# Attention layers of a four-layer graph network: probabilities turned by transfers inside SBUF and VectorE block transposes, contexts one slot later

## The chip, the cores and the metric

One core of a Trainium2 chip runs the whole program in one launch. The metric is the device time of that launch in microseconds, lower is better. The kernel before takes 2639.49 us, the median of 3 runs (2638.67 to 2640.51). The core has TensorE (PE; its weight loads are PEld), VectorE (DVE), ScalarE (ACT), GpSimd (POOL), and SyncE (SP), which issues nearly all transfers. Each engine works through its own instructions in order, and they meet at semaphores.

## The reference

The input is x of 128 graphs with 64 nodes and 384 features in float32, and an adjacency matrix of 64 x 64 for each graph. Four layers follow each other, each as x = layernorm(x + layer(x)). The first two are graph convolutions and stay as they are. The third and the fourth are the attention layers with 12 heads of 32 features:

```python
# third layer
q = (x @ Wq.T) ; k = (x @ Wk.T) ; v = (x @ Wv.T + bv)          # split in 12 heads
a = einsum('bnhd,bmhd->bhnm', q, k) * 384**-0.5 + adj[:, None]
pad = all(a == 0, axis=-1)                                     # rows that are all zero give zero
a = nan_to_num(softmax(where(pad, -inf, a)))
out = einsum('bhnm,bmhd->bnhd', a, v).reshape(...) @ Wo.T + bo
# fourth layer
q = x @ Wq + bq ; k = x @ Wk + bk ; v = x @ Wv + bv            # split in 12 heads
s = q k^T / sqrt(32) + beta * adj ; s = where(adj > 0, s, -9e15)
out = softmax(s) @ v
```

## The kernel before

`heads_pass` computes both attention layers as one pipeline of 32 slots. A slot is a group of 8 graphs, that is 512 rows in 4 tiles t of 128 rows; slots 0 to 15 are the third layer (`project(n)` is true, because that layer has the output projection Wo), slots 16 to 31 the fourth. There are three chunks c of 128 features, four heads each, and six units k of scores (`UNITS`), two for a chunk. Products that need full precision are done as three float32r products of high and low parts (`hhi`, `hlo`, `whi`, `wlo`).

For one slot: 54 matmuls of 128x512 make queries and keys (`query_key(n, k)`, k = 0 to 5: even k are queries, odd k are keys, in two ring banks of PSUM); 36 matmuls make the values (`value(n, t)`) in the same two ring banks; `chunk_scores(n, c)` makes the scores of four heads in a pair of banks. VectorE adds the adjacency while it takes the scores out, and reduces them to row maxima (`maxima`, L1725 to L1733); GpSimd subtracts these (`take_off`, L1890); ScalarE takes the exponential (`exponential`, L1619). TensorE turns the probabilities with six transposes for each tile (`probs_turned`, L1495) into two banks, ScalarE copies them to SBUF (`probs_out`, L1633), and TensorE multiplies them with the values (`output`, L1509), a column of ones giving the sums. VectorE divides (`divide`, L1766 to L1770). In the third layer the contexts are turned (`outputs_turned`), split into high and low parts and multiplied with Wo (`result`), and `result_out` adds them to the rows of x; then mean, variance and the final scaling follow (`final_stats`, `final_power` on GpSimd, `final_shift`, `final_apply` on ScalarE), and SP stores the rows.

The order of the work is written out by hand for each engine, in one loop over the slots n. On TensorE a slot holds: values of slot n, with the turned contexts of slot n-1 in between; the last chunk's scores of slot n; the Wo products of slot n-1; then the queries and keys of slot n+1, and between them the transposes, the contexts of slot n and the first two chunks' scores of slot n+1. VectorE takes the values out with their bias (`values_out`, 16 additions of 64x192 in a slot, L1745), turns the next strip of x with a block transpose (`rows_turned`, L1710), and does what is named above. ScalarE takes queries and keys out of PSUM (L1604, L1606, L1609) and makes the high parts (L1596); GpSimd makes the low parts (`low_parts`, L1897) and adds the bias or the contexts to the rows of x (`residual`, L1904, L1907). SP's queue holds for each slot: load of x, two loads of the adjacency, four loads of strips (each into 32 partitions, L1383), and the store of the slot before.

The rule for a new query projection is in its first wait; a bank of the ring is free again when the values of tile 2 (k = 0) or 3 (k = 1) have been taken out:

```python
            if k >= 2:
                pe.wait_ge(qk_evac, 2 * KC * n + k - 1)
            elif project(n - 2):
                pe.wait_ge(w_evac, T * (n - 2) + (1, 4)[k])
            else:
                pe.wait_ge(v_evac, max(T * (n - 1) + 3 + k, 0))
```

Of the kernel before, what the change touches and what calls it, by code (L numbers as in the profile page):

```python
# [13 lines left out]
P = 128  # L14
S = 64
# [1248 lines left out]
def heads_pass(nc, sh, ctx, rows, groups, x_ins, strip_ins, x_outs, adj_d, rowvec_d, colvec_d, beta_d):  # L1264
# [48 lines left out]
    q = sb("q", [P, KC, R])  # L1313
    keys = sb("keys", [P, KC, GRAPHS, 2, S])
    z = [sb(f"z{a}", [P, T, D]) for a in "ab"]
    at_low += [sh.rows_at + (KC * R + KC * GRAPHS * 2 * S + 2 * T * D) * 4]
    xt += [sb("xtb", [P, KC, R])]
    hlo = [placed(at)(f"hlo{a}", [P, KC, R], F32R) for at, a in zip(at_low, "ab")]
    logits = sb("logits", [P, KC, HP, T, S])
    val = sb("val", [P, GRAPHS, PAIRS, 2, HO])  # L1320
    sb = placed(sh.rows_end_at)
    rowvec = sb("rowvec", [P, 3, D])
    adjp = [sb(f"adjp{a}", [P, T, S]) for a in "ab"]
    probs = [sb(f"prob{a}", [P, KC, T, HP, S]) for a in "ab"]
    probt = [sb(f"probt{k}", [P, PAIRS, P]) for k in range(2)]
    o = sb("o", [P, T, D])
    at_ohi = sh.rows_end_at + (3 * D + 2 * T * S + 2 * KC * T * HP * S + 2 * PAIRS * P + T * D) * 4
# [3 lines left out]
    off = sh.stage[1][:, 0, 0:T * S].rearrange("p (t j) -> p t j", t=T)  # L1331
    pt, ot, ring = sh.bank[0:2], sh.bank[2:4], sh.bank[4:6]
    scores = sh.pair[:, :].rearrange("p (h t j) -> p h t j", h=HP, t=T)
    FV, FR, FB = (small[:, k, :] for k in range(3))

    output_banks = (pt[0], pt[1], ot[0], ot[1])
    result_banks = (ring[0], ot[1], ot[0], ring[1])
# [19 lines left out]
    exp_done = sem("exp_done")  # L1357
    pt_done = sem("pt_done")
    pt_evac = sem("pt_evac")
# [17 lines left out]
    def sync_program(sync):  # L1377
# [11 lines left out]

        def load_adj(n):  # L1390
            for b in range(2):
                sync.dma_start(adjp[n % 2][S * b:S * b + S, :, :], adj_d[b][n % groups])\
                    .then_inc(adj_loaded[n % 2], 16)
# [23 lines left out]
        load_x(1)  # L1417
        yield
# [12 lines left out]
        store(slots - 1)  # L1431
# [3 lines left out]
    def tensor_program(pe):  # L1435
        def query_key(n, k):
# [3 lines left out]
            elif project(n - 2):  # L1440
                pe.wait_ge(w_evac, T * (n - 2) + (1, 4)[k])
            else:
                pe.wait_ge(v_evac, max(T * (n - 1) + 3 + k, 0))
# [26 lines left out]
        def chunk_scores(n, c):  # L1470
            pe.wait_ge(qk_evac, 2 * KC * n + 2 * c + 2)
            pe.wait_ge(s_evac, UNITS * n + 2 * c)
            for t in range(T):
                for b in range(2):
                    g, out = 2 * t + b, slice(S * b, S * b + S)
                    for r in range(2):
                        heads = slice(S * r, S * r + S)
                        mm = nc.tensor.matmul(scores[out, 2 * r:2 * r + 2, t, :], q[heads, c, g * S:(g + 1) * S],  # L1478
                                              keys[heads, c, g, :, :],
# [3 lines left out]
        def probs_turned(n, t):  # L1483
            prob = probs[n % 2]
            pe.wait_ge(exp_done, UNITS * n + 2 * KC - 1 + t // 2)
            for half in range(2):
                if t:
                    pe.wait_ge(pt_evac, 2 * (T * n + t) - 1 + half)
                else:
                    pe.wait_ge(pt_evac, 2 * T * n)  # L1490
                    if project(n - 1):
                        pe.wait_ge(olo_done, T * (n - 1) + half + 1)
                for j in range(PAIRS // 2):
                    m = PAIRS // 2 * half + j
                    mm = nc.tensor.transpose(pt[half][:, j * P:(j + 1) * P],  # L1495
                                             prob[:, m // 2, t, m % 2 * 2:m % 2 * 2 + 2, :].rearrange("p h j -> p (h j)"),
                                             sh.ident[:, :])
                mm.then_inc(pt_done, 1)

# [622 lines left out]
```

## Time and profile before

| | |
|---|---|
| median of 3 runs | 2639.49 us |
| the profiled execution | 2636.74 us, its span 2634.8 us |
| TensorE matmuls | 2568.1 us busy, 97% of the span, 23040 matmuls |
| TensorE weight loads | 2234.6 us, 85% |
| VectorE | 2010.6 us, 76% |
| ScalarE | 1220.0 us, 46% |
| GpSimd | 1525.9 us, 58% |
| SP's DMA queue | 253008 packets, 184.21 MB, 25.6% of 16 DMA engines |
| granted TensorE clock, mean | 0.993 |

The profile is of one execution. Busy times of the engines lie beside each other. Matmuls are pipelined, so the modelled end of one lies beyond the start of the next, and the distance between two starts tells what one costs in a row of them. An idle time stands in square brackets with what ended it. A clock of 1.00 is 2.4 GHz, one of 0.50 is 1.2 GHz; a value between them is a mean over both levels. The attention layers take the last 1065 us of the span.

### The profile page before, as it was taken

The numbers are of one execution on the slowest core, as the hardware profiler recorded it, in microseconds if no ns is written. First come the engines' busy times: TensorE is split into PE (matmuls) and PEld (weight loads), VectorE is DVE, ScalarE is ACT, GpSimd is POOL, SyncE is SP. The second block draws the span as 40 slices with busy tenths as digits, with TensorE's granted clock in tenths as the row PEclk, the third lists the DMA queues.
The fourth block names the chain that finished last, engine by engine and source line by source line (L and its number), as shares of the span: only waits on it lengthen the run. The fifth ranks groups of instructions, "written<-read, shape, count | busy, mean of one in ns | idle before, by whom it ended". The sixth has DMA issues, their size and how long they took to land.

```text
span 2634.8 us, 59176 instructions
## 1 busy us (share of the span) xinstructions
PE 2568.1 (97%) x23040; PEld 2234.6 (85%) x23040; DVE 2010.6 (76%) x4485; ACT 1220.0 (46%) x2385; POOL 1525.9 (58%) x1380
## 2 busy tenths in 40 slices
PE   7999999999998999999999998999999999999997
PEld 7998998998996788888888877888888888888886
DVE  5788888888887667666666758888888877777776
ACT  2344344444343344344344444555455555556554
POOL 7657657656757667666667656444434435555553
PEclk9999999999999999999999999999999999999999
DMA  5112112112125222222222223312333323333432
GB/s 161 35 43 63 64 43 71 56 45 68 52 54 169 50 65 60 61 61 73 61 54 64 61 60 104 77 52 65 77 77 77 76 61 84 87 77 89 103 77 75
DMA packets 253285, 187.97 MB, mean 71 GB/s; under 512 B 175568, under 2 KB 250960, under 8 KB 253008
## 3 DMA queue, kind: packets, MB, share of 16 engines
q1 hardware_dynamic: 253008, 184.21, 25.6%
q8 instruction: 183, 3.00, 0.5%
q14 instruction: 94, 0.77, 0.1%
HBM read 133.84 MB, written 50.33 MB: 70 GB/s over the span
## 4 chain that ended last, share of the span: by engine, by line
PE 92%; DVE 3%; issue 2%; POOL 1%; ACT 1%; DMA 0%; POOLq 0%; ACTq 0%; DVEq 0%
PE bank L1449 15%; PE bank L344 14%; PE bank L1457 12%; PE bank L888 12%; PE pair L888 11%; PE pair L1478 4%; PE bank L1509 4%; PE bank L1495 4%; PE bank L326 3%; PE pair L326 3%; PE bank L359 2%; PE bank L874 2%; PE bank L912 2%; PE pair L912 2%; PE bank L374 1%
## 5 line engine op out<-in xcount | busy, mean ns | idle before, releaser
L1890 POOL TENSOR_TENSOR h_logits<-h_logits,h_mx 128x512 f32<-128x512 f32 x192 | 202.4, 1055 | 267.1 <-DVE h_mx L1733 267.1
L1745 DVE TENSOR_TENSOR h_val<-bank,h_rowvec 64x192 f32<-64x192 f32 x512 | 181.8, 355 | 33.3 <-PE bank L1457 24.4
L1185 POOL TENSOR_TENSOR l_hlo<-l_hf,l_hhi 128x576 fp32r<-128x576 f32 x96 | 134.8, 1433 | 115.0 <-ACT l_hhi L1005 115.0
L412 ACT ACTIVATE l_sides<-bank 128x512 f32<-128x512 f32 x192 | 113.0, 595 | 177.9 <-PE bank L344 177.9
L1449 PE MATMUL bank<-h_hhia,whi 128*128 128x512 f32 x450 | 185.9, 413 | 3.4 <-DVE h_hloa L1716 2.3
L1449 PE MATMUL bank<-h_hhia,wlo 128*128 128x512 f32 x450 | 177.4, 394 | 0.0
L1609 ACT ACTIVATE h_keys<-bank,h_keycol,h_halves 128x512 f32<-128x512 f32 x192 | 138.9, 776 | 83.0 <-PE bank L1449 83.0
L1082 DVE TENSOR_TENSOR l_val<-bank,l_vec 64x384 f32<-64x384 f32 x256 | 142.3, 556 | 40.3 <-PE bank L888 37.3
L1082 DVE TENSOR_TENSOR l_val<-pair,l_vec 64x384 f32<-64x384 f32 x256 | 142.3, 556 | 32.0 <-PE pair L888 28.3
L1224 POOL TENSOR_TENSOR l_vdiag<-l_vdiag,l_vec 128x384 f32<-128x384 f32 x128 | 127.8, 1019 | 66.0 <-ACT l_vdiag L986 66.0
L888 PE MATMUL bank<-whi,l_hhi 128*128 128x384 f32 x576 | 141.2, 353 | 5.8 <-POOL wlo L74 5.8
L1633 ACT ACTIVATE h_probt<-bank 128x384 f32<-128x384 f32 x256 | 111.5, 490 | 67.6 <-PE bank L1495 67.5
L663 POOL TENSOR_TENSOR l_small<-l_small,power 128x4 f32<-128x4 f32 x32 | 32.4, 1014 | 180.3 <-DVE l_small L524 180.3
L1005 ACT ACTIVATE l_hhi<-l_hf 128x576 fp32r<-128x576 f32 x96 | 58.6, 673 | 162.3 <-PE pair L888 159.2
L1733 DVE TENSOR_REDUCE h_mx<-h_logits 128x8 f32<-128x512 f32 x192 | 130.8, 681 | 3.3
L888 PE MATMUL pair<-whi,l_hhi 128*128 128x384 f32 x576 | 130.8, 334 | 1.5 <-DVE l_val L1082 1.5
L888 PE MATMUL bank<-wlo,l_hhi 128*128 128x384 f32 x576 | 131.8, 336 | 0.0
L888 PE MATMUL bank<-whi,l_hlo 128*128 128x384 f32 x576 | 131.3, 335 | 0.0
L888 PE MATMUL pair<-whi,l_hlo 128*128 128x384 f32 x576 | 131.0, 334 | 0.0
L888 PE MATMUL pair<-wlo,l_hhi 128*128 128x384 f32 x576 | 130.7, 334 | 0.0
L888 PEld LDWEIGHTS bank<-whi,l_hhi 128*128 128x128 f32 x576 | 97.4, 189 | 30.6 <-issue 18.6
L1509 PEld LDWEIGHTS bank<-h_val,h_probt 128*64 128x64 f32 x3072 | 95.2, 137 | 22.7 <-issue 22.7
(268 smaller groups left out, 7723.2 us busy)
## 6 DMA issues: line engine op xcount, KB each, us to landing
h_strips<-x SPq DMA_DIRECT2D x128, 192.0 KB, 5.1
l_hf<-xt SPq DMA_DIRECT2D x16, 864.0 KB, 4.7
l_x<-x SPq DMA_DIRECT2D x32, 384.0 KB, 3.2
h_za<-x SPq DMA_DIRECT2D x16, 768.0 KB, 4.8
h_zb<-x SPq DMA_DIRECT2D x16, 768.0 KB, 5.1
l_x<-x SPq DMA_DIRECT2D x15, 768.0 KB, 4.6
x<-l_zfa SPq DMA_DIRECT2D x8, 768.0 KB, 3.5
x<-l_zfb SPq DMA_DIRECT2D x8, 768.0 KB, 4.3
```

What stands on the lines that cost most here:

```text
L326: mm = nc.tensor.matmul(value_bank(n, k)[:, 0:D], hh[:, c, k * P:(k + 1) * P], ww[:, c, :], start=(j == 0), stop=(j == len(terms) - 1))
L344: mm = nc.tensor.matmul(ring[k % RING][:, :], ww[:, c, m * P:(m + 1) * P], hh[:, c, :], start=(j == 0), stop=(j == len(terms) - 1))
L888: mm = nc.tensor.matmul(ring[k % RING][:, 0:D], hh[:, c, first:first + P], ww[:, c, :], start=(j == 0), stop=(j == len(terms) - 1))
L1082: ins = nc.vector.tensor_tensor(val[half, (g + b) % GRAPHS, 0:D], ring[k % RING][half, 0:D], bias[half, :], ALU.add)
L1185: nc.gpsimd.tensor_tensor(hlo[:, c, :], hf[:, c, :], hhi[:, c, :], ALU.subtract).then_inc(lo_done, 1)
L1449: mm = nc.tensor.matmul(ring[k % 2][:, :], ww[:, c, m * P:(m + 1) * P], hh, start=(c == 0 and j == 0), stop=(c == KC - 1 and j == 2))
L1457: mm = nc.tensor.matmul(out, lhs, rhs, start=(j == 0), stop=(j == len(terms) - 1))
L1509: mm = nc.tensor.matmul(ot[t % 2][rows, 2 * m * HO:2 * (m + 1) * HO], probt[t % 2][:, m, rows], val[:, 2 * t + b, m, :, :].rearrange("p h ...
L1609: ins = nc.scalar.activation(keys[:, c, :, h, :], ring[1][:, :].rearrange("p (g j) -> p g j", j=S), ACT.Identity, scale=halves[:, h:h + 1] ...
L1733: nc.vector.tensor_reduce(mx[:, c, :, ts], row, AX.X, ALU.max)\
L1745: ins = nc.vector.tensor_tensor(val[S * p:S * p + S, 2 * t + b, :, p, 0:HD], src[rows, :, p, :], bias[rows, :, p, :], ALU.add)
L1890: nc.gpsimd.tensor_tensor(row, row, mx[:, c, :, ts].unsqueeze(3).broadcast_to([P, HP, 2, S]), ALU.subtract).then_inc(sub_done, 1)
```

## The change

The probabilities are no longer turned on TensorE. Scores, logits and adjacency get another layout: a row's 64 columns are split into two halves of 32, and the columns are laid out as (pair m, piece v, tile t, 32). The exponentials are written over the logits (there are two logits buffers now, and no `probs`). When all six exponentials of a slot are done, SP issues 16 transfers from SBUF to SBUF (`load_pieces`): each moves the 32x32 blocks of one of four groups of 32 partitions and one of four pieces (32 partitions, 6 x 128 float32 in a partition). VectorE then turns the blocks with four block transposes of 128x768 (`probs_turned`), which write `probt` for all four tiles.

The contexts of slot n are made at the start of slot n+1, all four tiles in a row in four banks, and the last chunk's scores of slot n+1 come right behind them, ahead of its values. Queries and keys of two chunks at a time are held instead of three. The values are taken out of PSUM by ScalarE without a bias, 16 copies a slot; the bias is added by GpSimd (`outputs_in`, to the contexts in the third layer, and `biases`, to the rows of x). GpSimd subtracts the maxima in two halves for each unit. The strips are turned one slot earlier (`rows_turned(n + 2)`) and so loaded one earlier; the adjacency is loaded in four parts.

```diff
+        def load_pieces(n):
+            sync.wait_ge(exp_done, UNITS * (n + 1))
+            sync.wait_ge(pt_done, T * n)
+            for v in range(STRIPS):
+                for w in range(P // SQ):
+                    sync.dma_start(pieces[SQ * v:SQ * v + SQ, w, :, :, :].rearrange("p m t a -> p m (t a)"),
+                                   logits[n % 2][SQ * w:SQ * w + SQ, :, v, :, :].rearrange("p m t a -> p m (t a)"))\
+                        .then_inc(pieces_loaded, 16)
...
         for n in range(slots):
-            if n >= 2:
-                load_x(n)
             if n and n + 1 < slots:
                 sync.wait_ge(s_evac, UNITS * n)
                 load_adj(n + 1)
-            if n + 2 < slots:
-                sync.wait_ge(xt_done, n + 2)
-                load_strips(n + 2)
+            load_pieces(n)
+            if n + 3 < slots:
+                sync.wait_ge(xt_done, n + 3)
+                load_strips(n + 3)
             if n:
                 store(n - 1)
+                if n + 1 < slots:
+                    load_x(n + 1)
...
         def output(n, t):
-            pe.wait_ge(pt_evac, 2 * (T * n + t + 1))
+            pe.wait_ge(pt_done, T * n + t + 1)
             pe.wait_ge(v_evac, T * n + t + 1)
...
         for n in range(slots):
             before, more = project(n - 1), n + 1 < slots
             if n:
+                for t in range(T):
+                    output(n - 1, t)
+                chunk_scores(n, 2)
                 value(n, 0)
...
             value(n, 2)
             value(n, 3)
-            chunk_scores(n, 2)
+            if n == 0:
+                chunk_scores(0, 2)
...
             if more:
                 query_key(n + 1, 0)
                 query_key(n + 1, 1)
-            if not before and more:
+                chunk_scores(n + 1, 0)
                 query_key(n + 1, 2)
-            probs_turned(n, 0)
...
                 query_key(n + 1, 3)
-            output(n, 0)
-            output(n, 1)
-            if more:
                 chunk_scores(n + 1, 1)
...
                 query_key(n + 1, 4)
-            probs_turned(n, 3)
-            if more:
                 query_key(n + 1, 5)
-            output(n, 2)
-            output(n, 3)
+        for t in range(T):
+            output(slots - 1, t)
```

The new order on ScalarE, GpSimd and VectorE (lines of the new loop; `alone` is true for n up to 16):

```python
        for n in range(slots):                    # ScalarE
            if n:
                exponential(n, 2)
                exponential(n, 3)
                if more and not alone:
                    high_parts(n + 1)
                values_out(n, 0)
            if before:
                outputs_high(n - 1, range(0, 2))
            if n:
                values_out(n, 1)
                exponential(n, 4)
            if before:
                outputs_high(n - 1, range(2, 4))
            values_out(n, 2)
            if n:
                exponential(n, 5)
            values_out(n, 3)
            if more and alone:
                high_parts(n + 1)
            if n == 0:
                for k in range(2, UNITS):
                    exponential(0, k)
            if more:
                query_key(n + 1, 0)
                query_key(n + 1, 1)
            if n:
                final_apply(n - 1)
            if more:
                query_key(n + 1, 2)
                query_key(n + 1, 3)
                exponential(n + 1, 0)
                exponential(n + 1, 1)
                query_key(n + 1, 4)
                query_key(n + 1, 5)

        for n in range(slots):                    # GpSimd
            if n and more and not alone:
                low_parts(n + 1)
            if n:
                outputs_in(n - 1)
            take_off(n, 4)
            take_off(n, 5)
            if n and more and alone:
                low_parts(n + 1)
...
            if n:
                final_power(n - 1)
            biases(n)
            if more:
                for k in range(4):
                    take_off(n + 1, k)
```

On VectorE a slot is now: the four divisions of slot n-1, two units of maxima, `outputs_low`, `rows_turned(n + 2)`, `result_out`, the final statistics, two units of maxima of slot n+1, and then in the third layer the four block transposes and two more units of maxima, in the fourth layer the two units first and the transposes after them.

## Rows read from the trace of the kernel before

**Rows 1.** Page, part 1: busy time, share of the span, instructions of each engine.
```profile
PE 2568.1 (97%) x23040; PEld 2234.6 (85%) x23040; DVE 2010.6 (76%) x4485; ACT 1220.0 (46%) x2385; POOL 1525.9 (58%) x1380
```

**Rows 2.** Windows, fourth layer: length, busy time of each engine, clock, DMA share, GB/s.
```profile
2200.00:2400.00 200.00, 200.00 (x2146) 169.47 (x2145) 153.41 (x351) 117.66 (x212) 105.67 (x98) 1.00 0.35 89
```

**Rows 3.** Timeline of TensorE: start, length (us), engine, line, operation, tiles, shape, count.
```profile
1629.48 0.80 PE L1457 MATMUL bank<-whi,h_hhia 128*128 128x384 f32 x3
...
1665.32 0.80 PE L1457 MATMUL bank<-whi,h_hhia 128*128 128x384 f32 x3
...
2202.92 0.80 PE L1457 MATMUL bank<-whi,h_hhia 128*128 128x384 f32 x3
...
2229.86 1.63 PE L1509 MATMUL bank<-h_val,h_probt 128*64 128x66 f32 x48
2231.41 0.80 PE L1457 MATMUL bank<-whi,h_hhib 128*128 128x384 f32 x3
...
2238.19 1.10 PE L1478 MATMUL pair<-h_keys,h_q 64*64 64x128 f32 x32
2239.22 0.50 PE L1449 MATMUL bank<-h_hhia,whi 128*128 128x512 f32 x1
```

**Rows 4.** Timeline of all engines, around a key projection in the third layer.
```profile
1760.13 0.64 PEld L1495 LDWEIGHTS bank<-ident,h_proba 128*128 128x128 f32 x6 [0.17 <-issue]
...
1762.47 0.39 PE L1449 MATMUL bank<-h_hlob,whi 128*128 128x512 f32 x1
...
1762.70 0.40 PE L1449 MATMUL bank<-h_hhia,wlo 128*128 128x512 f32 x1
...
1763.13 1.45 ACT L1609 ACTIVATE h_keys<-bank,h_keycol,h_halves 128x512 f32<-128x512 f32 x2 [1.48 <-PE bank L1449]
...
1764.63 1.10 PE L1478 MATMUL pair<-h_keys,h_q 64*64 64x128 f32 x32
```

**Rows 5.** Timelines of ScalarE and GpSimd, start of a fourth-layer slot.
```profile
2202.47 1.44 ACT L1609 ACTIVATE h_keys<-bank,h_keycol,h_halves 128x512 f32<-128x512 f32 x2
...
2203.30 1.99 POOL L1907 TENSOR_TENSOR h_za<-h_za,h_o 128x384 f32<-128x384 f32 x2 [3.56 <-DVE h_o L1770]
2205.55 3.79 POOL L1897 TENSOR_TENSOR h_hloa<-h_xta,h_hhib 128x512 fp32r<-128x512 f32 x3 [0.25 <-ACT h_hhib L1596]
```

**Rows 6.** Groups of instructions: busy us, mean ns of one, idle before and its releaser.
```profile
L1633 ACT ACTIVATE h_probt<-bank 128x384 f32<-128x384 f32 x256 | 111.5, 490 | 67.6 <-PE bank L1495 67.5
L1619 ACT ACTIVATE h_probb<-h_logits 128x512 f32<-128x512 f32 x96 | 58.9, 633 | 50.3 <-POOL h_logits L1890 49.7
L458 ACT ACTIVATE l_e<-l_ut 128x256 f32<-128x256 f32 x32 | 13.4, 418 | 148.2 <-DVE l_ut L504 148.2
L1890 POOL TENSOR_TENSOR h_logits<-h_logits,h_mx 128x512 f32<-128x512 f32 x192 | 202.4, 1055 | 267.1 <-DVE h_mx L1733 267.1
L629 POOL TENSOR_TENSOR l_maska<-l_adjna,tri 128x256 f32<-128x256 f32 x16 | 12.2, 763 | 0.0
L1710 DVE STREAM_TRANSPOSE h_xta<-h_strips 128x1536 f32<-128x1536 f32 x7 | 12.4, 1768 | 0.0
```

**Rows 7.** Second layer: two waits in TensorE's timeline, and windows behind them.
```profile
858.00 0.53 PE L374 MATMUL bank<-l_val,l_dt 64*64 64x385 f32 x1 [1.72 <-DVE l_dt L510]
...
885.50 0.53 PE L374 MATMUL bank<-l_val,l_dt 64*64 64x385 f32 x1 [3.59 <-DVE l_dt L510]
...
858.00:865.00 7.00, 7.00 (x40) 5.12 (x41) 4.54 (x19) 3.19 (x7) 1.02 (x1) 1.00 0.19 41
885.50:892.00 6.50, 6.50 (x31) 4.17 (x32) 3.90 (x16) 2.35 (x5) 1.02 (x1) 0.74 0.59 133
```

**Rows 8.** Line L1383: issue time in ns (min/median/max), and time to landing.
```profile
L1383 SPq DMA_DIRECT2D h_strips<-x x128: 303/546/2590, 1527.6 to 2551.6; - x128
...
DMA to landing us min/median/max: 2.9/5.1/6.8
```

**Rows 9.** Timeline of TensorE, entry to the attention layers.
```profile
1605.80 1.99 PE L1478 MATMUL pair<-h_keys,h_q 64*64 64x128 f32 x32 [5.51 <-DVE h_logits L1725]
```

More of the change, by code:

```diff
@@ L1330, in heads_pass @@
     olo = sb("olo", [P, T, KC, P], F32R)
-    off = sh.stage[1][:, 0, 0:T * S].rearrange("p (t j) -> p t j", t=T)
-    pt, ot, ring = sh.bank[0:2], sh.bank[2:4], sh.bank[4:6]
-    scores = sh.pair[:, :].rearrange("p (h t j) -> p h t j", h=HP, t=T)
+    off = sh.stage[1][:, 0, 0:T * S]
+    output_banks, ring = sh.bank[0:4], sh.bank[4:6]
+    scores = sh.pair[:, :].rearrange("p (m v t a) -> p m v t a", m=2, v=STRIPS, t=T)
     FV, FR, FB = (small[:, k, :] for k in range(3))
-    output_banks = (pt[0], pt[1], ot[0], ot[1])
-    result_banks = (ring[0], ot[1], ot[0], ring[1])
     vec_in = sem("vec_in")
@@ L1654, in scalar_program @@
             exponential(0, k)
-        high_parts(1)
-        for a in range(2):
-            act.wait_ge(rows.stored[a], 16 * (groups // 2))
         for n in range(slots):
             before, more = project(n - 1), n + 1 < slots
+            alone = n <= groups
             if n + 1 == groups:
@@ L1870, in vector_program @@
                 final_shift(n - 1)
+            else:
+                for a in range(2):
+                    dve.wait_ge(rows.stored[a], 16 * (groups // 2))
             if more:
@@ L1878, in vector_program @@
                 maxima(n + 1, 3)
-        divide(slots - 1, 2)
-        divide(slots - 1, 3)
+            if not project(n):
+                for t in range(T):
+                    probs_turned(n, t)
+        for t in range(T):
+            divide(slots - 1, t)
         final_stats(slots - 1)
@@ L1919, in gpsimd_program @@
         take_off(0, 3)
+        pool.wait_ge(vec_in, 16 * 3)
         for n in range(slots):
-            before, more = project(n - 1), n + 1 < slots
+            more, alone = n + 1 < slots, n <= groups
+            if n and more and not alone:
+                low_parts(n + 1)
             if n:
-                residual(n - 1, range(T // 2, T))
-            if n and more:
-                low_parts(n + 1)
+                outputs_in(n - 1)
             take_off(n, 4)
             take_off(n, 5)
+            if n and more and alone:
+                low_parts(n + 1)
             split_weights(sh, pool, "lo", *weights_of_slot(n))
@@ L1930, in gpsimd_program @@
                 final_power(n - 1)
+            biases(n)
             if more:
-                take_off(n + 1, 0)
-                take_off(n + 1, 1)
-            residual(n, range(T // 2))
-            if more:
-                take_off(n + 1, 2)
-                take_off(n + 1, 3)
-        residual(slots - 1, range(T // 2, T))
+                for k in range(4):
+                    take_off(n + 1, k)
+        outputs_in(slots - 1)
         final_power(slots - 1)
```

282 lines of the change are left out of this document (121 added, 161 removed).

## The prediction

> **What bounds the kernel now.** The page comes first: TensorE is busy 97% of the span, VectorE 76%, GpSimd 58%, ScalarE 46% [rows 1]. The windows view of a stretch of the attention layers shows TensorE busy 200.00 of 200 us at a clock of 1.00 (2.4 GHz), VectorE 153, ScalarE 118, GpSimd 106 [rows 2]. So a slot of these layers lasts as long as its matmuls, and whatever leaves TensorE's order shortens it, provided that nothing else makes TensorE wait. The third view is TensorE's timeline: from one slot's first value product to the next are 35.84 us in the first attention layer (1629.48 to 1665.32) and 28.49 us in the second (2202.92 to 2231.41) [rows 3]. Slots 1 to 16 give 16 periods of the first kind (slot 16 still finishes the first layer's last group), slots 17 to 30 give 14 of the second. I forecast slot by slot, from who must hand TensorE what.
>
> **What leaves TensorE.** Six transposes of the probabilities take 0.64 us [rows 4]; there are four such sixes in a slot: -2.6 us. Eight copies at 0.49 us leave ScalarE [rows 6], nothing waited for them there but the turned pairs, so they give nothing more.
>
> **What the new order adds on TensorE: two waits per slot.** Before, between the keys' projection and the scores that use them stood transposes, contexts or the next query projection. Now `chunk_scores(n+1,0)` follows `query_key(n+1,1)` directly, and `chunk_scores(n+1,1)` follows `query_key(n+1,3)`. The price stands in the old trace: the last matmul of a key projection is issued at 1762.70, ScalarE copies the keys from 1763.13 for 1.45 us, and the scores start at 1764.63; in between TensorE did a pair of contexts [rows 4]. The next instruction could have gone at 1762.93, since these matmuls follow each other every 0.23 us (1762.47 to 1762.70); with nothing to do TensorE loses 1.7 us. TensorE's queue is in order, so everything behind the scores waits too. Two of them: +3.4 us. The scores of chunk 2 have the contexts ahead of them and wait for nothing new.
>
> **First layer's slots.** -2.6 + 3.4 = +0.8 us. I looked for a third wait, counting from the slot's first context. VectorE's divisions and two units of maxima end near 9.1, GpSimd's bias additions (4 at 1.0 [rows 5]) near 6.3, before TensorE needs the turned contexts at 8.2; values reach ScalarE at 6.2, 8.5, 10.7, 12.3 and it hands them on by 14.4; the low parts of the next strip end near 18.9, where TensorE asks for the last third at 19.8. None is late, by 1 to 2 us. 16 periods: +13 us.
>
> **Second layer's slots: a chain.** Count from the moment when TensorE reaches `output(n-1,0)`. It has four contexts (3.1 us, twice the 1.55 from 2229.86 to 2231.41), chunk 2's scores (1.03) and four value products (6.78) before the next slot's first query projection [rows 3]: 10.9. The block transposes pace the contexts: half of a 1.77 us transpose is 0.89, with a fixed part 0.97 [rows 6], against 0.78 for a context, and they run right before, so +0.4: 11.3. That projection must wait until ScalarE has taken the values of tile 2 out of the ring bank, and ScalarE's order puts `exponential(n,4)` ahead of that, GpSimd's order puts `low_parts(n+1)` and `outputs_in(n-1)` ahead of the subtraction that the exponential needs:
>
> - keys' copy, two exponentials, high parts on ScalarE and low parts on GpSimd: in the old trace 2202.47 to 2209.34, 6.9 us [rows 5]; they start 0.2 after the slot does: 7.1.
> - `outputs_in(n-1)`: two such additions took 1.99 us [rows 5], four are 4.0: 11.1.
> - `take_off(n,4)`, now two halves: whole it took 1.06 [rows 6], so at least 1.06; a 128x256 GpSimd operation took 0.76, so at most 1.5. I take 1.25, midway, since the halves keep the broadcast operand that made the whole cheap: 12.35.
> - the exponential, 0.63 [rows 6]: 13.0.
> - `values_out(n,2)`: four copies of 64x192. The trace has no such copy; 128x256 took 0.42, 128x384 0.49 [rows 6]. By their slope 0.38, and less back to back; I take 1.35 for four, bounds 1.2 and 2.0: 14.4.
>
> TensorE arrives at 11.3 and starts at 14.4: +3.1 us, 2.9 to 4.0 with the bounds. Behind this wait is the whole projection of the next slot.
>
> **The clock.** In the second layer TensorE waited 3.59 us and then 6.5 us were granted 0.74 on average, that is 3.4 us at 1.2 GHz; after a wait of 1.72 us the next 7 us stood at 1.00 [rows 7]. A wait of 3.1 us in each slot, with two of 1.7 behind it, is nearer the first. 3.4 us at half the clock lose 1.7 us.
>
> The Trainium skill ("TensorE: Matmul & The Clock Gate", "HAM oscillation") tells of a matmul loop that waits in every step and so begins every step at the low clock; the row with 3.59 us agrees for one wait. The same page ("A second HAM failure mode: psum-queue depth-cycling") adds that frequent short idles between matmul groups alone make the clock swing. By that the first layer's slots would pay too, against the row of 1.72 us; no stretch before has two such waits close together.
>
> Sum for a second-layer slot: -2.6 + 3.4 + 0.4 + 3.1 + 1.7 = +6.0 us; 14 periods: +84 us.
>
> **The transfers, costed at nothing.** Sixteen issues on SP, which has nothing else to do then; strips of the same kind took 0.55 us to issue (median) and 5.1 us to land [rows 8]: 16 x 0.55 + 5.1 = 13.9 us. The last exponential ends near 15.1 in a second-layer slot, so the pieces lie there at 29, and the outputs come at 34.5: 4.5 us of cover, with the first transpose off it. In the first layer the last exponential ends near 13.2, the pieces land at 27, VectorE comes to them at 29.4. Below: 16 x 0.30 + 2.9 = 7.7 us. Above nothing in the trace moves SBUF to SBUF; at 1.0 us each and 5.1 landing it is 21 us. Behind them on SP stand the strips two slots ahead, the store and the load of x, each with over 10 us until its use; the adjacency's four smaller loads come before them. VectorE gains 3.9 us of transposes a slot and loses sixteen bias additions; even without that loss its 153 us in 200 would become 25.7 of a slot's 28.5.
>
> **Ends.** The entry to the stage gets better: TensorE waited 5.51 us for VectorE at 1605.80 [rows 9] (and twice before), since scores stood behind the values' copies; now maxima come first, but the first keys' copy stands behind four exponentials and two new waits come in. By the same steps the first value product of slot 1 moves from 1629.48 to about 1626: -3 us. The tail gets longer: after the last exponential 8.7 us of issues, 5.1 to land and a transpose of 0.97, with nothing beside them, less the 6.8 us by which its scores now precede the values and some 2 us for the old transposes: +6 us.
>
> **Sum.** 84 + 13 - 3 + 6 = +100 us. The profiled execution took 2636.74 us (span 2634.8), which makes 2737; the median of the runs before is 2.75 us above it, so I expect 2739 us.
>
> **Rivals.**
> - *The clock stays up in the second layer.* For it: the wait of 1.72 us cost none. Against: 3.59 did. 24 us less: 2715. 17%.
> - *The clock falls in the first layer's slots as well*, from the two short waits with only chunk scores and two projections between. 1.7 us in 16 slots, up to twice: 2766 to 2793. 14%. This is what the skill's second rule would make of it.
> - *The transfers are late.* It decides from some 18 us between the last exponential and the last landing. At 1.0 us per transfer, 21 us: 2.6 us in each of 14 slots, about 0.5 in each of 16: 2783; far more if the engines move these small rows at a fraction of the rate. For it: 3072 rows of 512 bytes a slot, 1.6 MB. Against: the strips' rate and the idle SP. 9%.
> - *The values come in time*, because GpSimd's low parts or additions overlap more than their order says. Then only the waits for keys remain: 0.8 x 30 + 0.4 x 14 + 3 = +33: 2672. Against: a queue in order. 7%.
> - *Faster.* ScalarE is only half busy, and if it hands the keys over so early that TensorE's wait at the scores is below 1.3 us each, the slot is shorter than before; with the waits gone and the values in time it gains 2.6 x 30, less 3 + 6 for ends and pacing: 2570. Against: the copy can't start before the last matmul's end, and takes 1.45 us. 5%.
> - My own case: 47%; 1% for what I don't see.
>
> **Numbers.** Predicted 2739 us. The range 2695 to 2795 holds my case, the first two rivals and the transfers' case at its first price: some 85%. A difference under 0.2% (5 us) can't be told from none; the only case that crosses it is the last rival: faster 0.05, the same 0.02, slower 0.93.
>
> **What would show it.** The timeline of TensorE should have two waits of 1.5 to 1.7 us per slot in front of the scores, named for ScalarE and the keys, and in slots from 17 on a third of about 3 us in front of a query projection, named for ScalarE and the values; the granted clock in a window over the second layer below 1.00, over the first at 1.00; periods near 36.6 and 34.5 us. VectorE should not wait for the pieces' transfers. Wrong would be: periods under 28.5 and 35.8, waits at the contexts for a transpose that itself waits for a DMA, or block transposes well over 1 us.

## Result, and the profile after

The changed kernel takes 2739.81 us (median of 4 runs, 2737.55 to 2743.88) against 2639.76 before: 1.038 times as long, 95% interval 1.0367 to 1.0393. Predicted were 2739 us, range 2695 to 2795.

Page of the changed kernel, part 1, to set beside [rows 1], and windows of the first and the second attention layer, to set beside [rows 2]:

```profile
PE 2505.6 (92%) x22272; PEld 2167.7 (79%) x22272; DVE 1982.6 (72%) x4101; ACT 1288.8 (47%) x2641; POOL 1674.7 (61%) x1700
```
```profile
1850.00:2050.00 200.00, 182.27 (x1868) 159.06 (x1868) 164.28 (x292) 111.30 (x229) 107.64 (x132) 1.00 0.43 111
2250.00:2450.00 200.00, 161.88 (x1689) 134.19 (x1690) 120.48 (x228) 113.35 (x228) 116.76 (x143) 0.96 0.48 121
```

TensorE does 768 instructions less, and is no longer busy all the time: 18 us of 200 are idle in the first layer, 38 in the second, where the clock is below 1.00 as well. Its list of waits over these layers (engine, tile, line, whom it waited for: us in total, times, longest; the three largest) says for whom:

```profile
PE pair L1492 <- ACT h_keys L1593: 93.6, 60, 2.8
PE bank L1462 <- ACT h_val L1610: 47.4, 14, 3.4
PE bank L1506 <- DVE h_probt L1703: 13.8, 1, 13.8
```

Sixty waits of the scores for the keys, fourteen of a query projection for the copied values, one at the end for the turned probabilities. TensorE's timeline places them. Here are a first-layer slot (from contexts to contexts, 36.57 us) and the second layer, where the slot that starts at 2425.57 lasts 32.31 us and its neighbours 33.87:

```profile
1808.15 1.10 PE L1492 MATMUL pair<-h_keys,h_q 64*64 64x128 f32 x32 [1.54 <-ACT h_keys L1593]
1815.10 1.10 PE L1492 MATMUL pair<-h_keys,h_q 64*64 64x128 f32 x32 [1.54 <-ACT h_keys L1593]
1820.44 3.03 PE L1506 MATMUL bank<-h_val,h_probt 128*64 128x66 f32 x96
...
1857.01 3.03 PE L1506 MATMUL bank<-h_val,h_probt 128*64 128x66 f32 x96
...
2425.57 3.03 PE L1506 MATMUL bank<-h_val,h_probt 128*64 128x66 f32 x96
2439.66 0.50 PE L1462 MATMUL bank<-h_hhib,whi 128*128 128x512 f32 x1 [3.40 <-ACT h_val L1610]
...
2457.88 3.03 PE L1506 MATMUL bank<-h_val,h_probt 128*64 128x66 f32 x96
2471.95 0.69 PE L1462 MATMUL bank<-h_hhia,whi 128*128 128x512 f32 x1 [3.39 <-ACT h_val L1610]
```

What makes the values late is read from the chain of waits of that stretch (start, us, what was last):

```profile
2431.25 1.29 POOL h_hloa L1865
2432.55 3.88 POOL h_za L1884 x4
2436.42 1.15 POOL h_logitsb L1857 x2
...
2437.60 0.02 ACT h_logitsb L1602
...
2438.25 0.33 ACT h_val L1610
```

Low parts, four additions to the rows, a subtraction, an exponential, the values' copies: GpSimd's and ScalarE's order, one after the other, while TensorE stands. The transfers land in 2.2 us, but their issue on SyncE takes 10.4 us for sixteen. The rows show the issue at the end of the program, the block transposes behind it, and the list of transfers (KB each, median us to landing):

```profile
2705.07 10.36 SPq L1397 DMA_DIRECT2D h_pieces<-h_logitsb  x16
2717.08 3.56 DVE L1703 STREAM_TRANSPOSE h_probt<-h_pieces 128x768 f32<-128x768 f32 x4 [11.40 <-DMA h_pieces<-h_logitsb]
```
```profile
h_pieces<-h_logitsb SPq DMA_DIRECT2D x256, 96.0 KB, 2.2
```

This is the tail, the only place besides the entry where something waits for them. VectorE's list of waits names them at fourteen of its maxima too, up to 5.7 us each. But each of these ends 0.06 to 0.08 us after the scores that the maxima read, and the kernel asks there only for the transfers of an earlier slot; experiment 5 takes the transfers away and the slots stay as long.

### The profile page after: what moved, and what is told of

Read it like the earlier page. It is cut to its first block, busy times and chain, and to the rows that moved or that the text cites. A ratio compares the mean times of both kernels' runs of the same rounds, so it can differ in the third digit from the quotient of the medians.

```text
span 2735.8 us, 57977 instructions
## 1 busy us (share of the span) xinstructions
PE 2505.6 (92%) x22272; PEld 2167.7 (79%) x22272; DVE 1982.6 (72%) x4101; ACT 1288.8 (47%) x2641; POOL 1674.7 (61%) x1700
## 4 chain that ended last, share of the span: by engine, by line
PE 67%; issue 11%; POOL 10%; DVE 8%; ACT 3%; DMA 0%; SPq 0%; POOLq 0%; DVEq 0%; ACTq 0%
PE bank L344 14%; PE bank L1462 12%; PE bank L888 11%; PE pair L888 11%; PE bank L326 3%; PE pair L326 3%; PE pair L1492 2%; ACT h_keys L1593 2%; PE bank L359 2%; POOL h_logitsa L1857 2%; PE bank L874 2%; DVE h_rec L1745 2%; POOL h_logitsb L1857 2%; PE bank L912 1%; PE pair L912 1%
## 5 line engine op out<-in xcount | busy, mean ns | idle before, releaser
L1610 ACT ACTIVATE h_val<-bank 64x192 f32<-64x192 f32 x512 | 169.3, 331 | 86.5 <-PE bank L1470 80.2
L1857 POOL TENSOR_TENSOR h_logitsb<-h_logitsb,h_mx 128x256 f32<-128x256 f32 x192 | 113.6, 616 | 140.9 <-DVE h_mx L1723 138.7
L1492 PE MATMUL pair<-h_keys,h_q 64*64 64x128 f32 x3072 | 107.0, 277 | 101.0 <-ACT h_keys L1593 98.2
L1857 POOL TENSOR_TENSOR h_logitsa<-h_logitsa,h_mx 128x256 f32<-128x256 f32 x192 | 114.6, 621 | 124.0 <-DVE h_mx L1723 121.8
L1492 PEld LDWEIGHTS pair<-h_keys,h_q 64*64 64x64 f32 x3072 | 83.7, 134 | 130.3 <-ACT h_keys L1593 124.4
L663 POOL TENSOR_TENSOR l_small<-l_small,power 128x4 f32<-128x4 f32 x32 | 32.4, 1013 | 179.9 <-DVE l_small L524 179.9
L1462 PEld LDWEIGHTS bank<-h_hhia,whi 128*128 128x128 f32 x450 | 87.2, 194 | 69.2 <-ACT h_val L1610 25.9
L1713 DVE SCALAR_TENSOR_TENSOR h_logitsb<-pair,h_adjpb 128x512 f32<-128x512 f32 x96 | 65.4, 682 | 95.3 <-PE pair L1492 65.5
```

The costliest lines, as they stand in the source:

```text
L1462: mm = nc.tensor.matmul(ring[k % 2][:, :], ww[:, c, m * P:(m + 1) * P], hh, start=(c == 0 and j == 0), stop=(c == KC - 1 and j == 2))
L1492: mm = nc.tensor.matmul(scores[out, r, :, t, :], q[heads, turn, g * S:(g + 1) * S], keys[heads, turn, g, :, :].rearrange("p h (w a) -> p ( ...
L1610: ins = nc.scalar.activation(val[S * p:S * p + S, 2 * t + b, :, p, 0:HD], src[S * b:S * b + S, :, p, :], ACT.Copy)
L1857: ins = nc.gpsimd.tensor_tensor(row, row, mx[:, c, 2 * u + h, :].unsqueeze(1).unsqueeze(3) .broadcast_to([P, 2, T, SQ]), ALU.subtract)
```

## Experiments

The kernel before, measured again beside each group of runs, took 2639.1 to 2639.4 us. Intervals are of the ratio to it. The theory: the price is made by the order on TensorE and GpSimd (two waits for keys in every slot, one for values in the second layer, with the clock behind it), not by transfers or block transposes.

**1. Scores behind the next query projection.**

```
-  query_key(n+1, 0..1)  chunk_scores(n+1, 0)  query_key(n+1, 2..3)  chunk_scores(n+1, 1)  query_key(n+1, 4..5)
+  query_key(n+1, 0..2)  chunk_scores(n+1, 0)  query_key(n+1, 3..4)  chunk_scores(n+1, 1)  query_key(n+1, 5)
```

> Only TensorE's order: each of the two early chunks' scores stands one projection later, behind the next query projection, so ScalarE copies the keys beside it. If each slot of the changed kernel pays 3.4 us for the two waits on the keys (2 x 1.54 idle and what overlaps), 30 slots give 102 us back: first-layer period 36.57 to 33.2, second-layer period 33.87 to 30.5, total about 2638 us; the wait of 3.4 us for the values stays. Rival, the wait only moves (the shorter slot brings TensorE to the contexts before the block transposes are done): a new wait for VectorE at the contexts, and half or less of the gain, about 2690.

Measured 2671.14 us (ratio 1.0103 to 1.0134). Waits of TensorE in this kernel:

```profile
PE bank L1506 <- DVE h_probt L1703: 35.5, 16, 13.9
PE bank L1516 <- POOL h_o L1881: 35.5, 45, 1.1
PE bank L1462 <- ACT h_val L1610: 19.5, 14, 1.4
```

No wait for keys is left, the one for values has shrunk to 1.4 us and the clock no longer falls; second-layer slots take 29.13 us. In the first layer a slot still takes 36.37: TensorE now waits 2.4 us for the divided and biased outputs (35.5 us in 15 slots). In the second it waits 1.4 us for the turned probabilities. Theory and rival were half right each: the order is worth 69 us, and 33 more that the theory expected went into new waits.

**2. Subtractions ahead of the additions in second-layer slots.**

```
-  outputs_in(n-1)  take_off(n, 4)  take_off(n, 5)
+  take_off(n, 4)  take_off(n, 5)  outputs_in(n-1)      (GpSimd, slots behind the first layer)
```

> Only GpSimd's order, and only in second-layer slots: the two subtractions of the maxima stand ahead of the four additions of the contexts. If the values come late because the exponential ahead of them waits for these additions, the third wait (3.40 us idle) and the low clock behind it (some 1.5 us) go: second-layer period 33.87 to 28.9, 14 periods, total about 2671 us, clock 1.00 there. Rival, ScalarE's copies of 64x192 are slow in themselves: the wait shrinks by less than 1 us, total above 2725. Rival, the additions are now late for the statistics behind them: a wait of ScalarE's final scaling moves on to the query copies, total above 2700.

Measured 2676.21 us (1.0123 to 1.0153). Waits, and a window of the second layer:

```profile
PE pair L1492 <- ACT h_keys L1593: 93.5, 60, 2.7
...
PE bank L1462 <- ACT h_val L1610: 2.0, 12, 0.2
```
```profile
2300.00:2500.00 200.00, 178.22 (x1964) 148.58 (x1965) 138.49 (x256) 131.03 (x264) 135.90 (x168) 1.00 0.56 141
```

The values' wait is gone and the fall of the clock with it; a slot takes 29.09 us, and what is left above 28.5 is what the keys' waits (3.1 us) cost beyond the transposes saved. These two lines on GpSimd were worth 64 us.

**3. The wait filled.** 24 transposes of the identity into a free bank while TensorE waits for the values; nothing else is changed.

> 24 transposes of the identity into a bank that is free then, in each second-layer slot between the last value product and the next query projection; nothing uses them. They fill some 2.6 of the 3.4 us in which TensorE waits for the values. If the wait pulls the clock down and that costs 1.5 us in 12 of 14 slots, the clock stays at 1.00 and the period falls from 33.87 to 32.3: about 2721 us, though TensorE does more. Rival, the clock falls from the whole slot's waits or costs nothing: no change, 2740. Rival, the filling is longer than the wait: slower.

Measured 2723.31 us (1.0303 to 1.0334).

```profile
PE bank L1462 <- ACT h_val L1614: 10.8, 14, 0.8
```
```profile
2300.00:2500.00 200.00, 176.87 (x1879) 150.72 (x1878) 123.17 (x231) 116.25 (x235) 123.48 (x152) 1.00 0.49 124
```

The values come as late as ever, but TensorE is idle for 0.8 us at a time and the clock stays at 1.00: every second-layer slot takes 32.3 to 32.4 us, where 12 of 14 took 33.87. So the low clock costs 1.5 us a slot.

**4. Both orders.**

> The orders of the first two kernels of this set together. If the terms add, 102 + 69 us: first-layer period 33.2, second-layer period 25.5, total about 2569 us, 70 us below the kernel before the change. Rival, with the slot at 25.5 us the chain from the last exponential over 16 issues and the landing (12.6 us measured) to the first block transpose has no cover left: waits of TensorE for the transposes and of VectorE for the transfers, second-layer period 26.5 to 28, total 2583 to 2604.

Measured 2658.88 us (1.0054 to 1.0088), some 90 above the theory and 55 above the rival's range. The timeline of TensorE in a first-layer slot (36.37 us):

```profile
1828.35 0.55 PE L1516 MATMUL bank<-ident,h_o 128*128 128x128 f32 x3 [0.28 <-POOL h_o L1881]
1830.04 0.55 PE L1516 MATMUL bank<-ident,h_o 128*128 128x128 f32 x3 [1.14 <-POOL h_o L1881]
1833.46 0.55 PE L1516 MATMUL bank<-ident,h_o 128*128 128x128 f32 x3 [0.97 <-POOL h_o L1881]
```

and VectorE, then TensorE, at the head of a second-layer slot (28.20 us):

```profile
2302.02 0.69 DVE L1713 SCALAR_TENSOR_TENSOR h_logitsa<-pair,h_adjpa 128x512 f32<-128x512 f32 x1 [2.93 <-PE pair L1492]
2304.67 3.55 DVE L1703 STREAM_TRANSPOSE h_probt<-h_pieces 128x768 f32<-128x768 f32 x4
2305.69 3.50 PE L1506 MATMUL bank<-h_val,h_probt 128*64 128x66 f32 x96 [1.48 <-DVE h_probt L1703]
```

With the first two waits gone, others that had lain under them come out: in the first layer VectorE's divides stand behind 3.8 us of maxima, in the second its block transposes do, and these pace the contexts besides (3.50 us, not 3.03). The rival had the place right and the reason wrong: the transposes stand behind the maxima, which wait for scores until 2302.02, and not behind transfers.

**5. No transfers after the first slot.**

```
   def load_pieces(n):
+      if n: return
...
   def probs_turned(n, t):
-      dve.wait_ge(pieces_loaded, 16 * 16 * (n + 1))
+      dve.wait_ge(exp_done, UNITS * (n + 1))
...
```

The kernel leaves out the transfers of slots 1 to 31, so these slots compute with slot 0's probabilities; the order of every engine is kept. The maxima wait for the exponentials of an earlier slot where they waited for its transfers.

> The changed kernel with its sixteen transfers only in slot 0: later slots issue none, their block transposes wait for the exponentials instead and turn slot 0's probabilities again (later outputs are made from these). Everything else stays, the order of every engine too. Theory (the prediction's: in the slots the transfers cost nothing, only the tail waits for them, 10.4 of issue and 1 to 2.2 of landing): 2739.8 - 11 = 2728 us (2724 to 2732), periods 36.6 and 33.9 unchanged. Rival (the transfers cost time in the slots, through SyncE's queue or by contention on the memory): periods fall by 1 us or more, 2700 us or less.

Measured 2731.74 us (1.0333 to 1.0363). The periods stay at 36.55 and 33.9; the time from the last slot's start to the tail's contexts falls from 24.55 to 13.05 us:

```profile
2701.54 3.03 PE L1507 MATMUL bank<-h_val,h_probt 128*64 128x66 f32 x96
2714.59 3.50 PE L1507 MATMUL bank<-h_val,h_probt 128*64 128x66 f32 x96 [2.33 <-DVE h_probt L1705]
```

The total fell by 8.1 us and not by these 11.5: in its profile the first contexts start at 1636.29, 6.3 us later than in the changed kernel, though nothing ahead of them was changed (experiment 10 has more on this spread). So 496 of 512 transfers cost nothing in the changed kernel's slots, as the prediction put them; what they cost lies in the tail and at the entry.

**6. The block transposes ahead of the maxima** (on the kernel of experiment 4, second layer).

```
-  maxima(n+1, 2)  maxima(n+1, 3)  probs_turned(n, 0..3)
+  probs_turned(n, 0..3)  maxima(n+1, 2)  maxima(n+1, 3)
```

> Both earlier orders kept (scores behind the next query; the subtractions ahead of the additions), and in the second layer VectorE's four block transposes put ahead of the third and fourth maxima of the next slot. In that kernel (2658.9 us) each second-layer slot waits 1.48 us for the block transposes, which start 2.6 us after the pieces have landed (about 2302 against 2304.67), behind maxima that wait for scores until 2302.02. Theory (the order on VectorE makes the last wait): the wait goes, 14 slots by 1.5 = 21 us, so 2638 us (2634 to 2643), second-layer period 26.7. Rival (the sixteen transfers pace the slot: 12.0 us to the last exponential, 10.4 of issue, 2.2 of landing, 0.9 of the first transpose, and the maxima put behind delay the exponentials by 1.5 to 2 us): period 27.1 to 27.6, 2643 to 2651 us.

Measured 2667.44 us (1.0089 to 1.0119), slower than without; periods 28.4 to 29.4, but for the first (27.24) and one of 30.51.

```profile
PE bank L1462 <- ACT h_val L1610: 16.4, 13, 1.4
PE bank L1462 <- ACT h_q L1590: 13.0, 13, 1.1
```

TensorE's wait for the transposes is gone, but the theory's gain did not come. The rival's mechanism did, at a higher price than its 27.1 to 27.6 us: the maxima that moved back hold up the exponentials, which stand first in ScalarE's slot with the values' copies behind them, and VectorE now waits for the pieces ahead of its transposes (36.1 us in 12 slots). Experiment 11 shows this round in its rows.

**7. The divides ahead of the maxima** (first layer; the maxima 2 and 3, their subtractions and exponentials behind the divides). 


> Both earlier orders kept, and in first-layer slots the third and fourth maxima of the slot, their subtractions on GpSimd and their exponentials on ScalarE put behind the divides of the slot before. In that kernel (2658.9 us, first-layer period 36.4) TensorE waits 2.2 us a slot for GpSimd's addition to the outputs (31.9 us in 14 slots), because VectorE does 3.8 us of maxima between the block transposes and the first divide. Theory: those waits go, 16 slots by 2.1 to 2.2 = 34 us, so 2625 us (2619 to 2632), first-layer period 34.2. Rival (VectorE's own round, 83 per cent busy, is the bound of a first-layer slot): the wait moves to the block transposes ahead of the contexts and the period stays at 36 to 36.5, 2653 to 2662 us.

> The two VectorE orders together (transposes ahead of the maxima in the second layer, divides ahead of them in the first). Theory: they lie in different slots and add, 2658.9 - 21 - 34 = 2604 us (2597 to 2612), below the kernel before by 27 to 42 us. Rival (each only moves the wait): 2640 to 2660 us.

Measured 2760.23 us (1.0442 to 1.0473), a slot 42 to 43 us; with experiment 6 together 2768.15 (1.0472 to 1.0507). Waits of the first, those on one of the two logits buffers (the other's are as many):

```profile
PE pair L1492 <- DVE h_logitsa L1719: 40.3, 6, 6.7
```

I had overlooked that all scores go through one PSUM pair. The third chunk's scores stand right behind the contexts in TensorE's queue, and they wait until VectorE has read the second chunk from it: 6.7 us, with everything queued behind. The clock falls with it: a window of 1850 to 2050 shows 0.89.

**8. The high parts first on ScalarE** (experiment 6, and in second-layer slots `high_parts(n+1)` ahead of `exponential(n, 2)`).

> The kernel with both earlier orders and the second layer's block transposes ahead of the maxima, with one line more: in second-layer slots ScalarE makes the high parts of the next slot before the third and fourth exponentials, not after them. Without that line it took 2667.4 us with second-layer periods of 28.4 to 29.4: the wait for the block transposes was gone, but TensorE waited for ScalarE instead (33 us in all, for values and queries), whose first instructions of the slot now waited for the maxima put behind. Theory: with the high parts first ScalarE has work while the maxima are made, these waits go too, and the period falls to 26.7 to 27.2: 2658.9 - 14 to 21 = 2638 to 2645 us. Rival (GpSimd's round is the bound: subtractions, then low parts, then subtractions): the period stays at 28 to 29, 2657 to 2670 us.

Measured 2650.05 us (1.0027 to 1.0057), periods 27.2 to 28.3, two of 29.6 and a first one of 25.96.

```profile
PE bank L1462 <- ACT h_q L1590: 13.0, 13, 1.0
PE bank L1462 <- ACT h_val L1610: 8.1, 12, 1.1
```

About half of the theory's gain, counted from experiment 4; a wait of 1.0 us for a query's copy, which stands behind the last scaling of the rows, is left.

**9. The outputs turned later** (on the kernel of experiment 4, first layer; ScalarE and VectorE follow in the same order, and ScalarE's exponentials of the third chunk go behind the outputs).

```
-  value 0  outputs_turned 0, 1  value 1  outputs_turned 2, 3  value 2  value 3
+  value 0  value 1  outputs_turned 0, 1  value 2  outputs_turned 2  value 3  outputs_turned 3
```

> The kernel with both earlier orders (2658.9 us), and in first-layer slots TensorE turns the outputs later (values 0 and 1, outputs 0 and 1, value 2, output 2, value 3, output 3, before: value 0, outputs 0 and 1, value 1, outputs 2 and 3, values 2 and 3), with the copies on ScalarE in that order and the low parts of the outputs on VectorE in two pairs. The attempt to move the divides forward instead took 2760 us: TensorE's third scores wait for the third and fourth maxima (6.7 us a slot), since the one PSUM pair holds one chunk. Theory: the 2.2 us a slot for which TensorE waits for GpSimd's additions go, with no other order changed: first-layer period 34.2, 16 slots, 2625 us (2619 to 2633). Rival (VectorE's and GpSimd's round bounds a first-layer slot at 36 us): the wait moves to the low parts or the block transposes, 2653 to 2662 us.

Measured 2621.33 us (0.9920 to 0.9953): the first version below the kernel before. First-layer slots take 33.87 us:

```profile
1850.00:2050.00 200.00, 197.33 (x1963) 171.92 (x1962) 176.00 (x314) 121.16 (x247) 116.62 (x143) 1.00 0.48 120
```

TensorE is busy 197 of 200 us; VectorE, at 176, was not the bound.

**10. The first slot's transfers ahead of two weight loads** (on the changed kernel).

> The changed kernel (2739.8 us), with the last two weight loads of SyncE's queue behind the first slot's sixteen transfers instead of ahead of them. Theory: the transfers start when the last exponential of slot 0 ends (1611.5 us) and not at 1616.6, so the first contexts (1630.0) start about 5 us earlier, and everything after them: 2734.8 us (2733 to 2737). Rival: VectorE's maxima of slot 1 or TensorE's own queue is next to end, and less than 2 us comes of it: 2738 to 2740 us.

Measured 2736.66 us (1.0351 to 1.0382). The first contexts start at 1625.63 in its profile, 4.4 us before those of the changed kernel, but kernels whose entry is the same differ there too (1630.01, 1632.94 in experiment 2, 1635.29 in experiment 3). Counted from the same scores (1613.35 here, 1613.57 there) they come 4.2 us earlier, and their wait of 4.08 us is gone; one of 1.44 us for VectorE at the next scores is new. The median fell by 3.1 us: between theory and rival, and hardly more than the runs spread (2732.61 to 2736.89 here; the profiled run is the lowest), so the trace shows the wait go and the size of the gain stays uncertain.

**11. All orders that gained**, and ScalarE's last scaling split around the query and key copies in the second layer.

> All the orders that gained, in one kernel: both earlier orders, the outputs turned later in the first layer (2621.3 us so far), the second layer's block transposes ahead of the maxima with the high parts ahead of the exponentials (8.9 us in its own comparison), the first slot's transfers ahead of the last two weight loads (3.1 us), and one new line: in second-layer slots ScalarE's last scaling of the rows is split, two row blocks ahead of the third query copy and two behind the third key copy, since TensorE waited 1.0 us in each slot for that query copy behind all four. Theory: they lie in different slots and add, 2621.3 - 8.9 - 3.1 - 14 by 0.6 to 1.0 = 2595 to 2601 us, taken as 2598 (2592 to 2606), second-layer period 26.7 to 27.2. Rival (GpSimd's and VectorE's round holds the second-layer slots at 27.5 to 28): 2606 to 2614 us. Either way below the kernel before, 2639 us.

Measured 2606.39 us (0.9860 to 0.9893): 33 us below the kernel before, 0.4 us above the theory's range and inside the rival's. First-layer slots take 33.87, second-layer slots 27.1 to 28.5, but for the first of them (25.95).

```profile
PE bank L1463 <- ACT h_val L1612: 14.0, 14, 1.1
```

The wait for the query copy is gone, and one for the values' copy has grown from 8.1 to 14.0 us in its place. What sets these slots stands in SyncE's and VectorE's rows, the issue of a slot's sixteen transfers and the transposes that wait for them:

```profile
2350.34 10.71 SPq L1397 DMA_DIRECT2D h_pieces<-h_logitsb  x16
2362.70 3.56 DVE L1713 STREAM_TRANSPOSE h_probt<-h_pieces 128x768 f32<-128x768 f32 x4 [2.73 <-DMA h_pieces<-h_logitsb]
2377.74 11.56 SPq L1397 DMA_DIRECT2D h_pieces<-h_logitsa  x16
2405.99 11.09 SPq L1397 DMA_DIRECT2D h_pieces<-h_logitsb  x16
```

From one start of issue to the next are 27.40 and 28.25 us; less the time of the issue itself that is 16.69 both times, and in thirteen second-layer slots in a row it is 16.67 to 16.72, while the issue varies from 10.41 to 11.88. In the changed kernel the distance is 33.87 whether the issue takes 10.40 or 11.05. So with the transposes ahead of the maxima the transfers stand in a round that sets the slot: last exponential, sixteen issues, landing, transposes, the maxima behind them, subtractions, low parts, exponentials. In experiment 6 the same difference is 18.0. No run shortened the issue here, so what that would give is not shown.

## Why the prediction was right, step by step

The total was right to 1 us; that is in part two errors that cancelled. From the first value product of slots 1 and 17 (before: [rows 3]; after: 1636.66 and 2226.3), that of slot 31 (2601.93, 2697.56) and the span's end (2634.8, 2735.8):

| stretch | predicted | measured |
|---|---|---|
| entry, to slot 1 | -3 | +7.2 |
| first layer, slots 1 to 16 | +13 | +16.2 |
| second layer, slots 17 to 30 | +84 | +72.2 |
| tail | +6 | +5.4 |
| sum | +100 | +101.0 |

- **The waits for keys** were priced at 1.7 us each from [rows 4]; they are 1.54. A first-layer slot came to +0.73 (36.57 against 35.84; predicted +0.8): 0.3 less for the waits, and 2.35 instead of 2.6 us for the transposes, two small errors that cancel. The +16.2 are 11 from fifteen such slots and 5 from slot 1, which the entry disturbs.
- **The values' chain**: TensorE arrives 10.7 us after the slot's start and goes on at 14.09 (predicted 11.3 and 14.4). Its links came within 0.2 us of the estimates: subtraction 1.15 (1.25), four value copies 1.36 (1.35), additions 3.88 (4.0). Experiment 2 shows that the order on GpSimd makes it.
- **Pacing by block transposes**, +0.4, was wrong for this kernel: the keys' waits let VectorE run ahead, and the four contexts take 3.03 us. It shows only where those waits are gone (3.50, experiment 4). For the total it is of no weight: a TensorE that comes earlier to the values waits for them that much longer (3.40 us, for 3.1).
- **The clock**, +1.7: 1.5 us where it falls (experiment 3), in 12 of 14 slots, 1.3 on average. The clock (0.4 us a slot) and the keys' waits (0.3) are most of the 12 us by which the second layer was overestimated: a slot is +5.37 us with the fall and +3.81 without, 5.15 on average, for 6.0.
- **The first layer's clock**: the rival of 14% and the second rule of the Trainium skill ("TensorE: Matmul & The Clock Gate", "A second HAM failure mode: psum-queue depth-cycling") would have it fall with two short waits a slot. The window of 1850 to 2050 shows 1.00, with two waits of 1.54 us in each of its slots: in this trace such waits did not make the clock swing. The prediction weighed this rival without a row, since "no stretch before has two such waits close together". That was wrong. In the trace of the kernel before, waits of 1.50 and 1.26 us end at 790.76 and 795.38, and waits of 2.25 and 2.15 us at 818.26 and 823.80. Behind the first pair the clock stayed, behind the second it fell (the wait at 823.80, and windows from 795.38 and 823.80 on):

```profile
795.38:802.00 6.62, 6.62 (x33) 4.29 (x34) 6.41 (x13) 3.10 (x5) 4.08 (x3) 1.00 0.45 120
823.80 0.53 PE L374 MATMUL bank<-l_val,l_dt 64*64 64x385 f32 x1 [2.15 <-DVE l_dt L510]
823.80:830.00 6.20, 6.20 (x30) 4.05 (x31) 5.01 (x11) 1.75 (x4) 3.22 (x2) 0.72 0.43 137
```

  In length two waits of 1.54 us are nearer the first pair, so these rows spoke against the rival before the change was run. They don't say what decides.
- **The transfers** cost nothing in this kernel's slots (experiment 5). The tail was right in sum: 10.4 us of issue and 2.2 to land, for 8.7 and 5.1.
- **The entry** is the step that failed, hidden in the total by the second layer. I followed the scores and the maxima, and not SyncE's queue: the first slot's transfers stand there behind two weight loads that wait for GpSimd's split of the weights. Timeline of the changed kernel (the split, the last of the slot's exponentials, scores, the second load, the transfers, the contexts):

```profile
1610.86 5.22 POOL L74 TENSOR_TENSOR wlo<-stage,whi 128x1152 fp32r<-128x1152 f32 x2
1610.92 0.63 ACT L1602 ACTIVATE h_logitsa<-h_logitsa 128x512 f32<-128x512 f32 x1 [0.51 <-POOL h_logitsa L1857]
...
1613.57 1.10 PE L1492 MATMUL pair<-h_keys,h_q 64*64 64x128 f32 x32 [3.07 <-ACT h_keys L1593]
1616.10 0.37 SPq L82 DMA_DIRECT2D stage<-L_gnn_Wv  x1
1616.59 10.75 SPq L1397 DMA_DIRECT2D h_pieces<-h_logitsa  x16
...
1630.01 2.25 PE L1506 MATMUL bank<-h_val,h_probt 128*64 128x66 f32 x36 [4.08 <-DVE h_probt L1703]
```

  The exponentials end at 1611.55, the transfers start at 1616.59. TensorE's wait of 4.08 us at the contexts is made of these 5 us: in experiment 10, where the transfers go first, it is gone, and the time falls by 3.1 us, hardly more than the runs spread. The rest of the 10 us by which the entry was missed lies in earlier waits (3.07 above, where the first keys' copy stands behind four exponentials; 3.84 at 1604.08 for low parts, 2.76 at 1598.26 for VectorE) and in the spread of entries; no run took it apart.
- **The rival "faster"**, 2570 with all waits gone, supposed that nothing lies beneath them. Something did: taking both away gave 2658.9. "None is late, by 1 to 2 us" was true of a TensorE that is held up for 3.1 us a slot, and no longer true of one that isn't. Without any wait but 0.35 us a first-layer slot is 33.87, 1.97 below before: of the 2.6 us of transposes 0.35 goes into that wait, and where the other 0.3 goes I don't know.
- The last kernel's second-layer slots stay at 27.1 to 28.5 us, and don't repeat evenly; by the rows of experiment 11 that is because the transfers, costed at nothing and free in the changed kernel, are no longer covered there, and the slot follows the time of their issue.

## What to carry to other kernels

Taking work off the bounding engine pays only if the instructions that then follow each other there don't depend on each other through another engine: put something independent between producer and consumer, and re-sort every other engine's queue by when that one asks. A slack counted in a trace holds for the speed that the trace has; when a wait is taken away, count again for all engines, since those under it come out (a first-layer slot fell from 36.57 us to 36.37 by the first order alone, and to 33.87 with the one under it). And follow the DMA queue at the entry and the tail, where nothing covers it, and again whenever the slots get shorter: transfers that were free at 33.9 us a slot set the slots of 27 to 28.5 us, once the transposes stood ahead of the maxima.

## What the hardware showed that I had not expected

- After waits of the same length the clock did and did not fall. Windows of the changed kernel behind the waits of 3.40 us at 2439.66 and 3.39 at 2471.95:

```profile
2439.66:2446.00 6.34, 4.80 (x34) 3.66 (x38) 2.73 (x10) 4.53 (x9) 4.89 (x5) 1.00 0.47 108
```
```profile
2471.95:2478.00 6.05, 5.97 (x18) 4.44 (x18) 2.73 (x10) 2.66 (x7) 4.91 (x5) 0.72 0.45 104
```

  In 12 of 14 slots it fell (0.72 here), in 2 it did not. What decides between the two I did not find.
- Transfers inside SBUF of 96 KB (32 partitions of 3 KB) land in 2.2 us, against 3.7 for the strips from DRAM, twice as large, in the same kernel (5.1 before [rows 8]). But each takes SyncE 0.65 us to issue, so that sixteen are bound by issue (10.4 us); the block transposes start 1.65 us after its end.
